# How softmax inverses reach the row layout in an attention and expert kernel: one 128x8 transpose and a broadcast through DRAM in place of a widened transpose

## The chip, the core and the metric

One Trainium2 chip, one of its NeuronCores. The metric is the device time of one execution, in microseconds (us), median of several runs. The kernel before takes 1382.95 us (three runs, 1381.9 to 1384.7).

## The reference, cut to what matters

`x` is 8 batches of 512 tokens with 256 features. A layer norm is followed by two branches whose results are both added to `x`: a mixture of 32 experts, and a latent attention with 16 heads. Only the attention matters here:

```python
scores = einsum('bhqd,bhkd->bhqk', query, key) * scale      # causal
attn = softmax(scores, axis=-1)
out = einsum('bhqk,bhkd->bhqd', attn, value)                # value = norm_kv @ W_dv
return out.transpose(0, 2, 1, 3).reshape(B, S, NH * VD) @ W_o
```

The kernel multiplies by the latent `norm_kv` (64 wide) in place of the value, and folds `W_dv` and `W_o` into one matrix. The division by the sum of a row's exponentials is done after that product, so each head and query needs one number, 1 / (row sum).

## The kernel before, in words

**Stages.** `attention` projects all batches and then runs `heads_first` on batches 0 to 3. `experts` follows, then `heads_last` on batches 4 to 7. The two head stages have the same build, in 32 pairs of heads each, and the change touches only them.

**A step.** Both stages run a pipeline of steps `g`, one head each, 16 to a batch, with `TAIL` = 6 more at the end. Every engine walks the same steps through its own `step` function, in an order written out by hand. `bt.back(g, lag)` names the head that was `lag` steps ago. There is no planner: an engine works through its own list, and a wait at its head holds all behind it.

- TensorE in step `g`: scores of query tile 3 (512 keys), in even steps the six matmuls of `queries` for the next pair, scores of tile 2, in odd steps `turn_norms` and `values` of the pair that ended two steps ago, scores of tile 1, then `turn` (ten 128x128 transposes of the head before, L1149 and L1587), scores of tile 0. In four even steps of a batch (4, 6, 12, 14) a `piece` of the output product with 24 matmuls runs first.
- VectorE: the four `maxima` of the step, and in even steps, between the first two, `between`: half of the rotated queries, `latent_norm` of the pair four steps ago (L1315, L1778), and the reciprocals `inverses` (L1303, L1766).
- ScalarE: the four `exps`, in even steps `queries_latent` behind the first of them (two 64x512 copies out of PSUM bank 0, L1217 and L1669, counted by `q_abs`), then the other copies.
- GpSimd: indirect DMAs (a scatter of token rows in the first stage, a gather with addition in the last). In the first stage also `latent_lo` (L1073).
- SyncE: the loads of the next batch's queries and latents and the stores of results (`during`). Behind batch 1 it also stores the weights (L1039 to L1041) and loads the first expert weights (L878, L879).

**The work around the change.** `rinv` holds the inverses as 128 queries x (2 heads, 4 query tiles). The product in PSUM, `o_ps`, has its rows by head and latent feature (2 x 64) and its columns by query (512), so the inverses must be turned and repeated over 64 rows. Before, GpSimd (first stage, L1078) or ScalarE (last stage, L1688) widens them to 128x512 in `spread`, TensorE turns `spread` with four 128x128 transposes (L1135, L1573) into bank 0, and ScalarE copies these 128x512 to `norms` (L1236, L1695). VectorE then multiplies `o_ps` by `norms`.

Bank 0 of PSUM is also where `queries` puts the first half of a pair's queries. So `turn_norms` waits until ScalarE has copied these out of it:

```python
pe.wait_ge(q_abs, min(NH * b + 2 * p + 6, NH * HB))
```

`2 * p + 6` is the count behind pair `p + 2`. Before, `turn_norms` of pair `p` runs in step `2p + 3`, one step after that copy.

## Time and profile before

| | |
|---|---|
| median of three runs | 1382.95 us |
| the profiled execution, its time and its span | 1381.9 us, 1381.9 us |
| TensorE busy | 1291.0 us (93%) |
| VectorE, ScalarE, GpSimd busy | 61%, 62%, 45% |
| `heads_first` | from 187.5 to 607.6 us |
| `experts` | from 608.6 to about 957 us |
| `heads_last` | from 957 us to the end |
| one pair of heads without a piece | 11.0 us |
| mean granted clock of TensorE | 0.981 of full speed |

The profile is of one execution, and all its times count from the span's start. Engines: PE is the matmul part of TensorE, PEld its weight loads, DVE VectorE, ACT ScalarE, POOL GpSimd, SP SyncE. An added q (SPq) marks what an engine's queue issues, as a DMA. A merged row of the timeline gives the start of its first instruction, the time that they cover, and their number.

### The profile page before, as it was taken

What the parts mean: (1) busy time and instruction counts of PE and PEld (TensorE: products, weight loads), DVE (VectorE), ACT (ScalarE), POOL (GpSimd) and SP (SyncE); (2) the same over time, 40 slices, a digit from 0 to 9 for tenths busy, and PEclk for the clock granted to TensorE, in tenths of its full rate; (3) what the DMA queues carried; (4) which work ended last, traced back from release to release, by engine and by line L of the source; (5) the groups of instructions that cost most, each with busy time, mean ns of one, the idle gap of its engine ahead of it and who ended that gap; (6) DMA issues with size and microseconds to landing.
All of it is one profiled execution on the core that took longest, in us unless ns stands there. A gap on an engine that the chain in (4) does not pass through costs nothing. (4 is left out here: it accounts for less than half of the span.)

```text
span 1381.9 us, 24599 instructions
## 1 busy us (share of the span) xinstructions
PE 1291.0 (93%) x7384; PEld 959.9 (69%) x7385; DVE 844.4 (61%) x3207; ACT 858.4 (62%) x2326; POOL 617.0 (45%) x542
## 2 busy tenths in 40 slices
PE   4999769999999999969999999997999999999997
PEld 3666446767777667757788888886667767777765
DVE  4587678777777677723333333333777777777774
ACT  1455427776677577635556656664777777777673
POOL 1111117777775777710000000001888888887820
PEclk9899979999999999999999999998999999999999
DMA  9977653333327422259976666664565665765510
GB/s 342 392 281 275 253 228 114 101 106 111 115 98 256 162 95 92 85 155 316 329 232 188 188 183 190 188 186 126 100 92 87 129 99 90 132 104 89 97 28 31
DMA packets 147284, 223.28 MB, mean 162 GB/s; under 512 B 13846, under 2 KB 128214, under 8 KB 142294
## 3 DMA queue, kind: packets, MB, share of 16 engines
q1 hardware_dynamic: 99350, 157.72, 33.9%
q0 software_dynamic: 36864, 53.50, 18.9%
q10 hardware_dynamic: 10944, 10.49, 2.6%
q8 instruction: 65, 1.06, 0.3%
q14 instruction: 61, 0.50, 0.1%
HBM read 105.27 MB, written 116.39 MB: 160 GB/s over the span
## 5 line engine op out<-in xcount | busy, mean ns | idle before, releaser
L1523 POOL DMA_INDIRECT l_sums<-sorted_y,slot_no x192 | 300.1, 1563 | 424.7 <-DMA l_sums<-base_dram 366.9
L1068 POOL DMA_INDIRECT sorted_x<-f_xn_row,slot_no x192 | 204.7, 1066 | 49.2 <-issue 44.5
L1224 ACT ACTIVATE f_prob<-f_prob,f_negmax 128x512 f32<-128x512 f32 (+3 forms) x256 | 142.6, 557 | 121.3 <-DVE f_negmax L1297 110.8
L2075 DVE SCALAR_TENSOR_TENSOR act_f<-hidden,rows_in,ps 128x96 f32<-128x96 f32 x224 | 70.5, 315 | 231.1 <-ACT hidden L2038 231.0
L1676 ACT ACTIVATE l_prob<-l_prob,l_negmax 128x512 f32<-128x512 f32 (+3 forms) x256 | 141.7, 555 | 104.9 <-DVE l_negmax L1760 97.2
L2000 PE MATMUL ps<-wgu_sb,xt_e 128*128 x896 | 184.2, 328 | 0.5 <-issue 0.4
L1565 PE MATMUL ps<-l_kt,l_qt 128*128 128x512 f32 (+3 forms) x512 | 170.5, 447 | 5.4 <-DVE l_qt L1751 4.8
L1127 PE MATMUL ps<-kt_s,f_qt 128*128 128x512 f32 (+3 forms) x512 | 170.8, 448 | 5.0 <-DVE f_qt L1288 4.4
L1297 DVE CUSTOM_DVE_ANT_0 f_prob<-ps,mask_add 128x512 f32<-128x512 f32 (+3 forms) x256 | 121.0, 486 | 83.5 <-issue 82.5
L1760 DVE CUSTOM_DVE_ANT_0 l_prob<-ps,mask_add 128x512 f32<-128x512 f32 (+3 forms) x256 | 121.0, 486 | 81.0 <-issue 79.7
L2000 PEld LDWEIGHTS ps<-wgu_sb,xt_e 128*128 128x128 f32 x896 | 139.9, 190 | 3.0 <-issue 2.0
L2018 PE MATMUL ps<-wd_sb,at 96*128 x448 | 139.3, 392 | 1.1 <-issue 0.6
L2046 ACT ACTIVATE rows_out<-ps 128x256 f32<-128x256 f32 x224 | 86.0, 384 | 81.4 <-PE ps L2018 81.3
L1127 PEld LDWEIGHTS ps<-kt_s,f_qt 128*128 128x128 f32 x512 | 82.7, 191 | 42.6 <-DVE f_negmax L1297 10.3
L1565 PEld LDWEIGHTS ps<-l_kt,l_qt 128*128 128x128 f32 x512 | 82.7, 191 | 42.5 <-DVE l_negmax L1760 11.9
L2033 ACT ACTIVATE xt_e<-ps 128x256 f32<-128x256 f32 x224 | 84.7, 378 | 19.2 <-PE ps L1989 19.1
L1989 PE MATMUL ps<-ident,rows_in 128*128 128x128 f32 x448 | 86.4, 274 | 7.6 <-DMA rows_in<-sorted_x 4.7
L2038 ACT ACTIVATE hidden<-ps 128x96 f32<-128x96 f32 x224 | 56.3, 251 | 51.4 <-PE ps L2000 51.4
L1989 PEld LDWEIGHTS ps<-ident,rows_in 128*128 128x128 f32 x448 | 62.1, 141 | 33.1 <-DMA rows_in<-sorted_x 8.2
L1587 PE MATMUL ps<-ident,l_prob 128*128 128x128 f32 x640 | 80.4, 273 | 1.6 <-ACT l_prob L1676 1.6
L1149 PE MATMUL ps<-ident,f_prob 128*128 128x128 f32 x640 | 80.4, 273 | 1.4 <-ACT f_prob L1224 1.4
L1149 PEld LDWEIGHTS ps<-ident,f_prob 128*128 128x128 f32 x640 | 73.9, 141 | 8.0 <-ACT f_pt L1230 1.6
(194 smaller groups left out, 2660.6 us busy)
## 6 DMA issues: line engine op xcount, KB each, us to landing
sorted_x<-zeros SPq DMA_DIRECT2D x14, 2304.0 KB, 9.8
rows_in<-sorted_x SPq DMA_DIRECT2D x112, 288.0 KB, 3.1
sorted_y<-rows_out SPq DMA_DIRECT2D x112, 256.0 KB, 2.1
wgu_sb<-in_wgu SPq DMA_DIRECT2D x16, 384.0 KB, 5.2
x_in<-in_x SPq DMA_DIRECT2D x8, 512.0 KB, 10.3
xn_dram<-xn SPq DMA_DIRECT2D x8, 512.0 KB, 4.0
base_dram<-x_in SPq DMA_DIRECT2D x8, 512.0 KB, 2.9
nqt_dram<-nqt_out SPq DMA_DIRECT2D x8, 512.0 KB, 3.9
```

Of the source, the lines that this page charges most:

```text
L1068: pool.indirect_dma_start(sorted_x, bass.IndirectOffsetOnAxis(ap=slot_no[:, t, k:k + 1], axis=0), xn_row[buf][:], None).then_inc(scattered ...
L1127: mm = pe.matmul(s_ps[k % 2][:, 0:w], qt[g // 2 % 2][g % 2][:, n * P:w], kt_s[:, b, 0:w], start=True, stop=True)
L1149: mm = pe.transpose(pt_ps[:, at:at + P], prob[:, g % 2, qt_no, kt_no * P:(kt_no + 1) * P], ident[:])
L1224: act.activation(prob[:, i, qt, 0:w], prob[:, i, qt, 0:w], ACT.Exp, bias=negmax[:, i, qt:qt + 1], scale=-1.0, accum_out=rowsum[:, g // 2 % ...
L1297: dve.tensor_tensor_reduce(prob[:, i, qt, 0:w], s_ps[k % 2][:, 0:w], mask[:, S - w:S], -1.0, -MASKED, ALU.add, ALU.min, negmax[:, i, qt:qt ...
L1523: pool.indirect_dma_start(sums[n % NSUM][:, t, :], None, sorted_y, bass.IndirectOffsetOnAxis(ap=slot_no[:, TT * GROUPS[n] + t, k:k + 1], a ...
L1565: mm = pe.matmul(s_ps[k % 2][:, 0:w], qt[g // 2 % 2][g % 2][:, n * P:w], kt[b - HB][:, 0:w], start=True, stop=True)
L1676: act.activation(prob[:, i, qt, 0:w], prob[:, i, qt, 0:w], ACT.Exp, bias=negmax[:, i, qt:qt + 1], scale=-1.0, accum_out=rowsum[:, g // 2 % ...
L1760: dve.tensor_tensor_reduce(prob[:, i, qt, 0:w], s_ps[k % 2][:, 0:w], mask[:, S - w:S], -1.0, -MASKED, ALU.add, ALU.min, negmax[:, i, qt:qt ...
L1989: mm = pe.transpose(xt_ps[par][:, kc * P:(kc + 1) * P], rows_in[j // 2 % AHEAD][:, par, kc * P:(kc + 1) * P], ident[:])
L2000: mm = pe.matmul(gu_ps[1 - par], xt[1 - par][:, kc, :], wgu_sb[kc][:, bass.ds(owner, 1), :].rearrange("p a f -> p (a f)"), start=kc == 0, ...
L2018: pe.matmul(y_ps[1 - par], at[1 - par][:], wd_sb[:, bass.ds(owner, 1), :].rearrange("p a h -> p (a h)"), start=True, stop=True)\
```

## The change

The inverses are turned as they are, `rinv` being 128x8, by one transpose into 8 partitions x 128 columns. ScalarE copies these to `inverse` (8 x 128). SyncE stores them in DRAM (4 KB), waits for the landing, waits until VectorE has read the `norms` of the pair before, and loads them with two broadcasting DMAs, 64 rows of 2 KB each, into `norms`. The widening is gone from GpSimd and from ScalarE. `turn_norms` stands one step earlier, in the even step behind the scores of tile 1 and ahead of `turn`. ScalarE's copy moves likewise, behind the third `exps` of the even step. SyncE's list is now written by steps, so its other DMAs have set places: the queries' loads in steps 5 and 13, the latents' in 11 and in 3 of the next batch, `x_res` in 15, the store of `res` in 7 of the next batch, and the stores of the weights with the first expert weights in step 7 of batch 2.

```diff
@@ both stages: tiles
-    spread = sb("f_spread", [P, 2, TT, 2, KVR])
+    inverse = sb("f_inverse", [2 * TT, 2, P])
-    norms_ps = ps[:, 0, :]
+    norms_ps = ps[0:2 * TT, 0, 0:P]
@@ both stages: SyncE, in place of during(b)
+            def spread_inverses(b, p):
+
+                sp.wait_ge(norms_copied, NP_ * b + p + 1)
+                sp.dma_start(norms_dram[p % 2], inverse[:, p % 2, :]).then_inc(norms_stored, 16)
+                sp.wait_ge(norms_stored, 16 * (NP_ * b + p + 1))
+
+                sp.wait_ge(lat_normed, NP_ * b + p)
+                for i in range(2):
+                    sp.dma_start(norms[i * KVR:(i + 1) * KVR, :].rearrange("r (t q) -> r t q", t=TT),
+                                 norms_dram[p % 2, i * TT:(i + 1) * TT, :].unsqueeze(0).to_broadcast([KVR, TT, P]))\
+                        .then_inc(norms_loaded, 16)
+
+            def step(bt, g):
+                b, p = bt.now, g // 2
+                if g % 2 == 0 and bt.back(g, 2):
+                    spread_inverses(bt.back(g, 2)[0], bt.back(g, 2)[1] // 2)
...
+                if bt.last is not None and g == 7:
+                    sp.wait_ge(res_added, 4 * bt.last + 4)
+                    sp.dma_start(base_dram[bass.ds(TT * bt.last, TT)].rearrange("t p h -> p t h"), res[:])\
+                        .then_inc(res_stored, 16)
+                if b == 2 and bt.last is not None and g == 7:
+                    for k in range(2):
+                        sp.dma_start(wq_dram[k], wq_s[k][:].bitcast(F32)).then_inc(kept, 16)
+                        sp.dma_start(wvo_dram[k], wvo_s[k][:].bitcast(F32)).then_inc(kept, 16)
+                    sp.dma_start(rope_dram, rope_t[:]).then_inc(kept, 16)
+                    for n in range(weights.EARLY):
+                        weights.load_chunk(sp, n, wgu, wd)
...
@@ GpSimd (first stage) and ScalarE (last stage): spread_inverses and its calls are gone
@@ both stages: TensorE
             def turn_norms(b, p):
 
                 pe.wait_ge(q_abs, min(NH * b + 2 * p + 6, NH * HB))
-                pe.wait_ge(spread_ready, NP_ * b + p + 1)
-                for t in range(TT):
-                    mm = pe.transpose(norms_ps[:, t * P:(t + 1) * P],
-                                      spread[:, p % 2, t].rearrange("p i n -> p (i n)"), ident[:])
-                mm.then_inc(norms_turned, 1)
+                pe.wait_ge(rinv_ready, NP_ * b + p + 1)
+                pe.transpose(norms_ps, rinv[:, p % 2].rearrange("p i t -> p (i t)"), ident[:]).then_inc(norms_turned, 1)
...
                 if par == 1 and bt.back(g, 3):
                     b, h = bt.back(g, 3)
-                    turn_norms(b, h // 2)
                     values(b, h // 2)
                 if g < NH:
                     scores(bt.now, g, 2)
+                if par == 0 and bt.back(g, 2):
+                    b, h = bt.back(g, 2)
+                    turn_norms(b, h // 2)
                 if bt.back(g, 1):
                     turn(*bt.back(g, 1))
@@ both stages: ScalarE
             def copy_norms(b, p):
 
                 act.wait_ge(norms_turned, NP_ * b + p + 1)
-                act.wait_ge(lat_normed, NP_ * b + p)
-                act.activation(norms[:], norms_ps, ACT.Copy).then_inc(norms_copied, 1)
+                if NP_ * b + p > 1:
+
+                    act.wait_ge(norms_stored, 16 * (NP_ * b + p - 1))
+                act.activation(inverse[:, p % 2, :], norms_ps, ACT.Copy).then_inc(norms_copied, 1)
@@ both stages: VectorE, latent_norm
-                dve.wait_ge(norms_copied, NP_ * b + p + 1)
+                dve.wait_ge(norms_loaded, 32 * (NP_ * b + p + 1))
```

## Rows read from the trace of the kernel before

**Rows 1.** The page's busy times: engine, us, share of the span, instructions.

```profile
PE 1291.0 (93%) x7384; PEld 959.9 (69%) x7385; DVE 844.4 (61%) x3207; ACT 858.4 (62%) x2326; POOL 617.0 (45%) x542
```

**Rows 2.** Busy time by stretch: PE, PEld, DVE, ACT, POOL, clock, DMA share, GB/s.

```profile
300.00:400.00 100.00, 100.00 (x597) 71.67 (x596) 76.25 (x282) 69.58 (x179) 74.17 (x82) 1.00 0.32 107
```

**Rows 3.** The timeline of PE in an odd step of the first stage.

```profile
343.54 0.81 PE L1127 MATMUL ps<-kt_s,f_qt 128*128 128x384 f32 x2
344.18 0.60 PE L1135 MATMUL ps<-ident,f_spread 128*128 128x128 f32 x4
344.71 2.37 PE L1164 MATMUL ps<-f_pt,f_nkv 128*64 128x512 f32 x16
```

**Rows 4.** The groups by line and form: count, busy us, mean ns, idle before.

```profile
L1149 PE MATMUL ps<-ident,f_prob 128*128 128x128 f32 x640 | 80.4, 273 | 1.4 <-ACT f_prob L1224 1.4
L1149 PEld LDWEIGHTS ps<-ident,f_prob 128*128 128x128 f32 x640 | 73.9, 141 | 8.0 <-ACT f_pt L1230 1.6
...
L1164 PEld LDWEIGHTS ps<-f_pt,f_nkv 128*64 128x64 f32 x512 | 34.3, 138 | 40.5 <-issue 36.0
```

**Rows 5.** The timeline of an even step of the first stage.

```profile
339.83 0.72 ACT L1224 ACTIVATE f_prob<-f_prob,f_negmax 128x512 f32<-128x512 f32 x1 [0.48 <-DVE f_negmax L1297]
...
340.55 1.19 ACT L1217 ACTIVATE f_qt<-ps 64x512 f32<-64x512 f32 x2
...
341.15 0.19 DVE L1303 RECIPROCAL f_rinv<-f_rowsum 128x8 f32<-128x8 f32 x1
...
341.36 1.25 PE L1149 MATMUL ps<-ident,f_prob 128*128 128x128 f32 x10
```

**Rows 6.** The timeline of the last stage's last even step with `queries`.

```profile
1340.74 1.19 ACT L1669 ACTIVATE l_qt<-ps 64x512 f32<-64x512 f32 x2
...
1341.54 1.25 PE L1587 MATMUL ps<-ident,l_prob 128*128 128x128 f32 x10
```

**Rows 7.** The timeline at the end of the first stage, where PE waits for ACT.

```profile
589.46 0.19 ACT L1224 ACTIVATION_READ_ACCUMULATOR f_prob<-f_prob,f_negmax 128x1 f32 x1
...
589.79 1.28 PE L1149 MATMUL ps<-ident,f_prob 128*128 128x128 f32 x10 [1.40 <-ACT f_prob L1224]
```

**Rows 8.** The timeline: the end of an even step's third `exps`, and the next pair's multiplication.

```profile
342.88 0.19 ACT L1224 ACTIVATION_READ_ACCUMULATOR f_prob<-f_prob,f_negmax 128x1 f32 x1
...
351.58 0.69 DVE L1315 TENSOR_TENSOR f_lat<-ps,f_norms 128x512 f32<-128x512 f32 x1
```

**Rows 9.** The DMA issues: count, KB each, median us to landing.

```profile
rows_in<-sorted_x SPq DMA_DIRECT2D x112, 288.0 KB, 3.1
sorted_y<-rows_out SPq DMA_DIRECT2D x112, 256.0 KB, 2.1
```

**Rows 10.** SP's queue, behind batch 1.

```profile
426.81 0.37 SPq L1033 DMA_DIRECT2D base_dram<-f_res  x1
...
437.01 3.43 SPq L878 DMA_DIRECT2D wgu_sb<-in_wgu  x2
...
441.99 1.57 SPq L1022 DMA_DIRECT2D f_nqt<-nqt_dram  x1
```

**Rows 11.** The timeline of batch 2: `turn` in step 6, `latent_norm` in step 10.

```profile
429.15 1.25 PE L1149 MATMUL ps<-ident,f_prob 128*128 128x128 f32 x10
...
450.40 0.69 DVE L1315 TENSOR_TENSOR f_lat<-ps,f_norms 128x512 f32<-128x512 f32 x1
```

**Rows 12.** Busy time by stretch, columns as in rows 2, as the weights' transfers end.

```profile
454.00:456.00 2.00, 0.20 (x1) 0.00 (x0) 2.00 (x8) 1.55 (x6) 1.67 (x3) 1.00 1.04 398
456.00:458.00 2.00, 1.30 (x8) 0.76 (x10) 1.08 (x2) 0.64 (x2) 1.67 (x4) 1.00 0.37 141
458.00:460.00 2.00, 2.00 (x10) 0.85 (x8) 0.00 (x0) 0.48 (x1) 1.60 (x2) 0.54 0.26 82
```

**Rows 13.** The waits from 440 to 470 us: total us, times, longest.

```profile
PE ps L1135 <- POOL f_spread L1078: 2.5, 1, 2.5
```

**Rows 14.** The timeline of the last stage's tail.

```profile
1363.40 0.20 DVE L1766 RECIPROCAL l_rinv<-l_rowsum 128x8 f32<-128x8 f32 x1 [0.52 <-ACT l_prob L1676]
```

More of the change, by code:

```diff
@@ new lines, in step @@
+            def step(bt, g):
+                b, p = bt.now, g // 2
+                if g % 2 == 0 and bt.back(g, 2):
+                    spread_inverses(bt.back(g, 2)[0], bt.back(g, 2)[1] // 2)
+                if b < HB - 1:
+                    if g == 5:
+                        sp.wait_ge(q_ready, 2 * (NP_ * b + QUART))
+                        sp.dma_start(nqt[0][:].bitcast(F32), nqt_dram[b + 1]).then_inc(nqt_loaded[0], 16)
+                    if g == 11:
+                        sp.wait_ge(pv_ready, NP_ * b + QUART)
+                        sp.dma_start(nkv[0][:], nkv_dram[b + 1]).then_inc(nkv_loaded[0], 16)
+                    if g == 13:
+                        sp.wait_ge(q_ready, 2 * (NP_ * b + NP_))
+                        sp.dma_start(nqt[1][:].bitcast(F32), nqt_dram[b + 1]).then_inc(nqt_loaded[1], 16)
+                    if g == 15:
+                        sp.wait_ge(res_added, 4 * b + 2)
+                        sp.dma_start(x_res[:], base_t[b + 1]).then_inc(xres_loaded, 16)
+                if bt.last is not None and g == 3:
+                    sp.wait_ge(pv_ready, NP_ * bt.last + NP_)
+                    sp.dma_start(nkv[1][:], nkv_dram[b]).then_inc(nkv_loaded[1], 16)
+                if bt.last is not None and g == 7:
[9 more added lines that the diff above has]
+                        weights.load_chunk(sp, n, wgu, wd)
@@ L1265, in step @@
                     exps(bt.now, g, 2)
+                if par == 0 and bt.back(g, 2):
+                    b, h = bt.back(g, 2)
+                    copy_norms(b, h // 2)
                 if bt.back(g, 1):
@@ L1506, in _, with spread_inverses @@
-            for b in range(HB, B - 1):
-                during(b)
+            def spread_inverses(b, p):
+                sp.wait_ge(norms_copied, NP_ * b + p + 1)
+                sp.dma_start(norms_dram[p % 2], inverse[:, p % 2, :]).then_inc(norms_stored, 16)
+                sp.wait_ge(norms_stored, 16 * (NP_ * b + p + 1))
+                sp.wait_ge(lat_normed, NP_ * b + p)
+                for i in range(2):
+                    sp.dma_start(norms[i * KVR:(i + 1) * KVR, :].rearrange("r (t q) -> r t q", t=TT),
+                                 norms_dram[p % 2, i * TT:(i + 1) * TT, :].unsqueeze(0).to_broadcast([KVR, TT, P]))\
+                        .then_inc(norms_loaded, 16)
@@ new lines, in step @@
+            def step(bt, g):
+                b, p = bt.now, g // 2
+                if g % 2 == 0 and bt.back(g, 2):
+                    spread_inverses(bt.back(g, 2)[0], bt.back(g, 2)[1] // 2)
+                if b < B - 1:
+                    if g == 5:
+                        sp.wait_ge(q_ready, 2 * (NP_ * b + QUART))
+                        sp.dma_start(nqt[0][:].bitcast(F32), nqt_dram[b + 1]).then_inc(nqt_loaded[0], 16)
+                    if g == 11:
+                        sp.wait_ge(pv_ready, NP_ * b + QUART)
+                        sp.dma_start(nkv[0][:], nkv_dram[b + 1]).then_inc(nkv_loaded[0], 16)
+                    if g == 13:
+                        sp.wait_ge(q_ready, 2 * (NP_ * b + NP_))
+                        sp.dma_start(nqt[1][:].bitcast(F32), nqt_dram[b + 1]).then_inc(nqt_loaded[1], 16)
+                if bt.last is not None and g == 3:
+                    sp.wait_ge(pv_ready, NP_ * bt.last + NP_)
+                    sp.dma_start(nkv[1][:], nkv_dram[b]).then_inc(nkv_loaded[1], 16)
+                if bt.last is not None and g == 7:
+                    store_out(bt.last)
@@ L1508, in _ @@
+            pipeline(step)(sp)
             store_out(B - 1)
@@ L1570, in turn_norms @@
                 pe.wait_ge(q_abs, min(NH * b + 2 * p + 6, NH * B))
-                pe.wait_ge(spread_ready, NP_ * b + p + 1)
-                for t in range(TT):
-                    mm = pe.transpose(norms_ps[:, t * P:(t + 1) * P],
-                                      spread[:, p % 2, t].rearrange("p i n -> p (i n)"), ident[:])
-                mm.then_inc(norms_turned, 1)
+                pe.wait_ge(rinv_ready, NP_ * b + p + 1)
+                pe.transpose(norms_ps, rinv[:, p % 2].rearrange("p i t -> p (i t)"), ident[:]).then_inc(norms_turned, 1)
             def turn(b, g):
@@ L1634, in step @@
                     b, h = bt.back(g, 3)
-                    turn_norms(b, h // 2)
                     values(b, h // 2)
@@ L1638, in step @@
                     scores(bt.now, g, 2)
+                if par == 0 and bt.back(g, 2):
+                    b, h = bt.back(g, 2)
+                    turn_norms(b, h // 2)
                 if bt.back(g, 1):
@@ L1727, in step @@
                     exps(bt.now, g, 2)
+                if par == 0 and bt.back(g, 2):
+                    b, h = bt.back(g, 2)
+                    copy_norms(b, h // 2)
                 if bt.back(g, 1):
```

85 lines of the change are left out of this document (17 added, 68 removed).

## The prediction, made before the changed kernel was run

> **What bounds the kernel now.** I read the page first: TensorE's matmul part is busy for 93% of the span [rows 1]. The busy time by stretch then shows that in the middle of a head stage it is busy for all of 100 us, at full clock, with every other engine below 77% [rows 2]. So in the steady part of both head stages only what stands in TensorE's own list costs time. Work taken from ScalarE or GpSimd gives nothing there, unless TensorE waits for it. The timeline of one odd and one even step then gives prices for what leaves and enters that list.
>
> **What is removed.** In an odd step the last matmul of the scores ahead, two of 0.32 each from 343.54, ends its streaming at 344.18. Four transposes follow, and `values` starts at 344.71: 0.53 us from start to start [rows 3]. Ten such transposes take 1.25 us with 273 ns for one alone [rows 4, 5], so in a row each costs (1.25 - 0.27) / 9 = 0.109 us, and four cost 0.44. The other 0.09 is the change to `values`' 64-column tiles, which stays. I take 0.44 (bounds 0.44 and 0.53). There are 32 pairs in each stage, and in two of the 64 the odd step belongs to a tail: 62 x 0.44 = 27.3 us less. The widening on GpSimd and ScalarE, and ScalarE's 128x512 copy lie beside TensorE: nothing.
>
> **What is added, and the wait that comes with it.** `turn_norms` now stands in the even step, in the place where `turn` starts today. It still waits for the count `2 * p + 6` of `q_abs`. Before, that copy was one step old. Now it is the copy of the same step: pair `p + 2` is the one whose queries TensorE has just computed. ScalarE's two copies end at 340.55 + 1.19 = 341.74, and `turn` starts at 341.36 [rows 5]: TensorE would come 0.38 us too early. In the last pair of the last stage it is 1340.74 + 1.19 - 1341.54 = 0.39 [rows 6]. Of the 60 pairs with a copy in such a step, all but one have 0.38 to 0.40. The copies can't come earlier: they stand behind the first `exps`, which waits for VectorE's maximum [rows 5], and that for the scores. The reciprocals are done at 341.34, ahead of the copies. Where TensorE does wait for ScalarE, it starts 589.79 - 589.65 = 0.14 us behind the release [rows 7]. The transpose itself then delays `turn` by its weight load, 0.14 [rows 4], since nothing runs that could cover it. Together 0.38 + 0.14 + 0.14 = 0.66 us for each of 60 pairs, 39.6 us; the two pairs without queries cost one transpose each, 0.2 in all. Bounds: 0.52 if the transpose is free, 0.79 if its whole 0.27 is exposed. The steady part so gives 39.6 + 0.2 - 27.3 = **+12.5 us** (between -1 and +21).
>
> Row and rule differ on that weight load. A load of 64 columns takes 138 ns and one of 128 takes 141 [rows 4], so for 8 columns I keep 0.14. The Trainium skill, "TensorE: Matmul & The Clock Gate", section "LDWEIGHTS (loading the stationary operand)", has it proportional to the columns. By that, 8 columns would cost nearly nothing; an estimate from it is 0.1 us less in each of 60 pairs, and a sum 6 us lower.
>
> **The new path of the inverses.** ScalarE's small copy would start when the third `exps` ends, 343.07 [rows 8]. It has a quarter of the columns of a 0.59 us copy; I take 0.25 (bounds 0.19, as for one column, and 0.59). SyncE then stores: 0.14 for the release and 2.1 to landing, loads: 0.14, the second issue 0.37, and 3.1 to landing [rows 9, 10]. That is 343.32 + 2.24 + 3.61 = 349.2. VectorE multiplies at 351.58 [rows 8]. So 2.4 us are left, and the trip is hidden (0), even though both prices are of transfers of 256 KB and more. Its cover is that slack; beyond it every microsecond stalls VectorE, behind which stand the other maxima, and so TensorE. GpSimd's transfers share the DMA engines; 256 KB per 11 us adds a few per cent.
>
> **SyncE's list.** Every other DMA of it moves to a set step. The loads of queries, latents and `x_res` come one to four steps later than today and are used steps after that: nothing. One place costs. In batch 2 the store of `res` and eleven large DMAs follow each other from 426.81; they are issued until 442 and single issues take over 1 us, where a free queue takes 0.37 [rows 10]. That is a queue filled to its end. It is drained at about 456.5 [rows 12]: 29.7 us for 7.9 MB, by the sizes of the tiles. In the changed kernel SyncE gets to them only behind the inverses of pair 2: `turn` at 429.15 [rows 11], the third `exps` ends 1.71 later as in rows 5 and 8, then copy, store and the issue of two loads, 434.1. Two loads (0.63 MB) are no longer in the block, so it takes 27.3 us, to 461.4. The store of pair 3's inverses is issued behind all that. I take it to land when the queue is empty, and the loads 3.6 later, at 465.0. They are due at 450.40 [rows 11]: TensorE stands for 14.6 us. Behind such a stop its clock falls: after today's short one it is 0.54 [rows 12], about 2 us lost. But today's stop, 2.5 us for GpSimd's late widening [rows 13] and its 2 us at the low clock, goes with the widening. So 14.6 + 2 - 4.5 = **+12 us** (lower bound -4, if the small store passes the block; upper +20).
>
> **Tails.** Reciprocals at 1363.60 [rows 14], transpose and copy to 1364.3, landing by the same prices at 1370.2; today VectorE multiplies at 1368.2, so up to 2 us, and about 1 in the first stage. The prices are for larger transfers, so I take half, **+1.5 us** (0 to 4).
>
> **Sum.** 1381.9 + 12.5 + 12 + 1.5 = 1407.9 us for the profiled execution. It was 1.05 below the median of the runs, so 1409.
>
> **Rivals.**
> - *The copies no longer arrive late: faster.* With 0.44 us less in each odd step the engines could settle so that `q_abs` is there in time. Then a pair gives 0.44 for 0.14 spent: 60 x 0.30 = 18 us less, and with 12 and 1.5 the time is 1378. It decides in the even step between the second scores and `turn`: the sum is a gain once TensorE's added time there is under 0.22 us in place of 0.66. For it: TensorE is the bound. Against it: the chain of scores, maximum, `exps`, copies has only idle time of 0.48 ahead of `exps` that its own maximum ends [rows 5], and it starts from TensorE's own scores, so it shifts with them. Chance 0.12.
> - *The trip through DRAM is longer than its cover: much slower.* If landing took 8.3 us from the copy on, in place of 5.9, every further microsecond would come 60 times; with loads of 6.2 us in place of 3.1, 0.7 x 60 = 42 us more, about 1450. For it: 64 rows read the same 2 KB of DRAM, which no row shows. Against it: the slack above. The Trainium skill, "DMA: Bandwidth & Descriptors", section "Rules for kernel authors", speaks against transfers under 64 KB as mostly overhead; it prices none that would outlast this slack. Chance 0.09.
> - *The wait costs 0.4 and the block nothing*, so that all cancels: 1383 to 1386. Chance 0.05.
>
> **Numbers.** The forecast has a chance of 0.72, and its own range is 1392 to 1425, from the bounds of the wait and of the block, not all at their ends together. Some 0.02 is for gains that I don't see. The range, 1376 to 1425, takes in the faster rival. A measurement here can tell about 0.2% from no change. Faster 0.14, within 0.2% 0.05, slower 0.81.
>
> **What would show it.** In the timeline of an even step: TensorE idle for some 0.5 us ahead of one transpose, released by ScalarE's `f_qt`; the stretch at 100 us no longer all busy; a pair at 11.2 us in place of 11.0. In batch 2: one stop of over 10 us in which VectorE waits for the load of `norms`, and a low clock behind it. No idle TensorE ahead of `turn_norms` would prove the steady part wrong; waits of `latent_norm` for DMAs in most pairs would mean the second rival; no long stop near 450 to 465 us would take 12 us off.

## The result, and the profile after

The kernel after takes 1406.56 us (median of four runs, 1405.16 to 1411.24), the kernel before, beside it, 1383.83 us (four runs, 1381.9 to 1387.33). The ratio is 1.0164, 95% interval 1.0142 to 1.0186: slower by 22.7 us. Forecast were 1409 us, in a range of 1376 to 1425. The profiled execution took 1405.44 us, with a span of 1403.7.

The page's busy times of the kernel after, beside [rows 1]:

```profile
PE 1283.7 (91%) x7193; PEld 930.6 (66%) x7193; DVE 847.1 (60%) x3207; ACT 826.4 (59%) x2294; POOL 593.9 (42%) x510
```

TensorE has 191 matmul records fewer, 32 x 2 x 3 = 192 being the transposes removed. Its work shrank and its time grew, so the new time is idle time. The busy time by stretch, for the window of [rows 2]:

```profile
300.00:400.00 100.00, 97.73 (x568) 66.68 (x567) 75.98 (x276) 66.27 (x177) 66.21 (x73) 1.00 0.37 128
```

In the stretch that was busy for 100 us, TensorE now stands for 2.3 us, at full clock. The timeline of an even step (the one of [rows 5]) shows where. Columns: start, us, engine, line, operation, tiles, count; in brackets the idle time ahead of it and its releaser.

```profile
341.31 1.19 ACT L1228 ACTIVATE f_qt<-ps 64x512 f32<-64x512 f32 x2
341.91 0.19 DVE L1316 RECIPROCAL f_rinv<-f_rowsum 128x8 f32<-128x8 f32 x1
...
342.55 0.08 PEld L1146 LDWEIGHTS ps<-ident,f_rinv 128*8 128x8 f32 x1 [0.67 <-ACT f_qt L1228]
342.55 0.27 PE L1146 MATMUL ps<-ident,f_rinv 128*8 128x128 f32 x1 [0.27 <-ACT f_qt L1228]
...
342.66 1.28 PE L1158 MATMUL ps<-ident,f_prob 128*128 128x128 f32 x10
```

The query copies end at 342.50, the inverses were ready at 342.10, and the transpose starts 0.05 behind the copies: the wait that was forecast, released by the engine that was forecast. PE's row shows only 0.27 us of idle time, because a record runs on past the place where the next matmul could start: in the kernel before, that of the scores ahead ends 0.17 behind the start of `turn` (341.53 and 341.36). Together 0.44, which to rounding is the 0.38 that TensorE would come too early and the 0.05 of the release. The waits of the whole kernel (total us, times, longest) count it in 59 of the 60 pairs that have a copy in that step:

```profile
PEld ps L1604 <- ACT l_qt L1700: 20.4, 30, 0.7
PEld ps L1146 <- ACT f_qt L1228: 19.4, 29, 0.7
DVE f_lat L1328 <- DMA f_norms<-norms_dram: 16.7, 2, 13.6
```

The third line is the stop in batch 2, with 3.1 us in the first stage's tail beside it; in no steady pair does VectorE wait for the DMA. The timeline of that stop, beside [rows 10, 11]:

```profile
448.47 1.26 SPq L880 DMA_DIRECT2D wd_sb<-in_wd  x1
449.77 1.48 SPq L1023 DMA_DIRECT2D norms_dram<-f_inverse  x1
462.66 1.09 SPq L1028 DMA_DIRECT2D f_norms<-norms_dram  x2
...
466.37 0.69 DVE L1328 TENSOR_TENSOR f_lat<-ps,f_norms 128x512 f32<-128x512 f32 x1 [13.63 <-DMA f_norms<-norms_dram]
...
467.31 0.37 PE L1146 MATMUL ps<-ident,f_rinv 128*8 128x128 f32 x1 [13.57 <-DVE f_rinv L1316]
```

The 4 KB store is issued as the last of the block. SyncE may issue the two loads only when it has landed, 12.9 us later, when the large transfers are through. VectorE stands for 13.63 us, TensorE for nearly as long. The busy time by stretch there, columns as in rows 2:

```profile
455.00:460.00 5.00, 0.00 (x0) 0.00 (x0) 0.00 (x0) 0.00 (x0) 2.91 (x3) 0.70 1.02 369
460.00:465.00 5.00, 0.00 (x0) 0.00 (x0) 0.00 (x0) 0.00 (x0) 3.36 (x5) 0.50 0.62 217
465.00:470.00 5.00, 2.69 (x13) 2.68 (x14) 1.64 (x8) 1.61 (x6) 0.00 (x0) 0.50 0.14 48
470.00:475.00 5.00, 5.00 (x27) 2.47 (x26) 4.03 (x15) 3.04 (x8) 0.85 (x1) 0.94 0.23 79
```

TensorE does nothing for 13.6 us, from 453.7 to 467.3, and comes back at half its clock (0.50, the 1.2 GHz level).

**The ledger.** I measure a pair from the end of ScalarE's second query copy to the next such end. The table has the most frequent value for pairs without a piece, "short pairs"; the others in this stage were 13.67 and are 13.80. From the first to the 32nd such end, the first stage is 15.4 us longer (378.0 to 393.4): 10.5 in the pair with the stop (28.68 for 18.0, where its like went from 13.67 to 13.80), 4.8 in all others. The last stage is 2.7 us longer (381.1 to 383.8), the time behind its last copy 4.3 (39.95 to 44.25). The rest, between and ahead of the stages, is 0.6 less. Together 21.8 us of span. In that rest stands `experts`, which neither the change nor any experiment touches: from its first matmul to its last it took 344.3 us before and 346.3 after, and 342.8 to 348.3 in the thirteen profiled executions. So the spans of two profiled executions can differ by some us for no reason of the edit, and the lengths of the pairs tell more.

### The profile page after: what moved, and what is told of

Read it like the earlier page. It is cut to its first block and busy times, and to the rows that moved or that the text cites. A ratio compares the mean times of both kernels' runs of the same rounds, so it can differ in the third digit from the quotient of the medians.

```text
span 1403.7 us, 24406 instructions
## 1 busy us (share of the span) xinstructions
PE 1283.7 (91%) x7193; PEld 930.6 (66%) x7193; DVE 847.1 (60%) x3207; ACT 826.4 (59%) x2294; POOL 593.9 (42%) x510
## 5 line engine op out<-in xcount | busy, mean ns | idle before, releaser
L1555 POOL DMA_INDIRECT l_sums<-sorted_y,slot_no x192 | 305.0, 1588 | 423.8 <-DMA l_sums<-base_dram 365.9
L1089 POOL DMA_INDIRECT sorted_x<-f_xn_row,slot_no x192 | 201.3, 1048 | 49.1 <-issue 44.5
L1094 POOL TENSOR_TENSOR f_lat_lo<-f_lat,f_lat_hi 128x512 fp32r<-128x512 f32 x32 | 48.3, 1509 | 83.5 <-ACT f_lat_hi L1254 83.4
```

Source lines behind the costliest of these rows:

```text
L1089: pool.indirect_dma_start(sorted_x, bass.IndirectOffsetOnAxis(ap=slot_no[:, t, k:k + 1], axis=0), xn_row[buf][:], None).then_inc(scattered ...
L1555: pool.indirect_dma_start(sums[n % NSUM][:, t, :], None, sorted_y, bass.IndirectOffsetOnAxis(ap=slot_no[:, TT * GROUPS[n] + t, k:k + 1], a ...
```

## The experiments

The kernel before, measured beside each group, had medians of 1383.8 us (the kernel after and experiments 1 to 4), 1383.5 (5 to 8), 1385.2 (9) and 1384.5 (10). Lengths of short pairs come from the traces.

| kernel | median us | ratio to before (95%) | short pair, first stage | last stage |
|---|---|---|---|---|
| before | 1383.8 | 1 | 11.03 | 11.02 |
| after | 1406.56 | 1.0164 (1.0142 to 1.0186) | 11.27 | 11.16 |
| the wait alone | 1407.89 | 1.0184 (1.0152 to 1.0216) | 11.52 | 11.52 |
| one transpose of four | 1372.58 | 0.9915 (0.9885 to 0.9944) | 10.92 | 10.79 |
| transpose behind `turn` | 1385.97 | 1.0011 (0.9994 to 1.0028) | 10.82 | 10.70 |
| block spread | 1393.12 | 1.0077 (1.0048 to 1.0107) | 11.27 | 11.16 |
| both repairs | 1371.72 | 0.9917 (0.9894 to 0.9940) | 10.83 | 10.70 |
| transpose inside `turn`, block spread | 1368.61 | 0.9894 (0.9872 to 0.9916) | 10.82 | 10.69 |
| before, block spread | 1385.17 | 1.0009 (0.9992 to 1.0026) | 11.03 | 11.02 |
| one transpose in the odd step, block spread | 1399.04 | 1.0098 (1.0059 to 1.0137) | 10.71 | 10.4 to 12.3 |
| `latent_lo` behind the scatters | 1426.36 | 1.0288 (1.0263 to 1.0313) | 11.16 or 11.27 | 11.16 |
| the same with the transpose inside `turn` | 1396.20 | 1.0079 (1.0062 to 1.0096) | 10.71 | 10.70 |
| a short `latent_lo`, block spread | 1390.07 | 1.0042 (1.0026 to 1.0059) | 11.16 | 11.16 |

### 1. The wait alone, in the kernel before

```diff
                 if g < NH:
                     scores(bt.now, g, 2)
+                if g > 1 and par == 0 and bt.next_pair(p):
+                    nb, np_ = bt.next_pair(p)
+                    pe.wait_ge(q_abs, NH * nb + 2 * np_ + 2)
                 if bt.back(g, 1):
                     turn(*bt.back(g, 1))
```

> The kernel before, and in it alone that TensorE waits, ahead of turn in every even step that has queries, for ScalarE's copies of these queries; it does nothing with what it waited for. Theory (the wait for q_abs is the price of the change): the copies end 0.38 us behind the place and the release costs 0.05 to 0.14, so 60 x 0.43 to 0.52 = 26 to 31 us more, about 1410 us, and a pair without a piece takes 11.5 us in place of 11.03. Rival (such a wait is absorbed by slack elsewhere, the loss comes from the DMAs): 1383 us, pairs at 11.0.

Measured: 24 us more than before, with nothing else changed, a little under the 26 to 31 expected. A pair costs 0.49 us more in both stages. The edit leaves out step 0 of each batch (`g > 1`), and there six pairs keep their 11.0 us; the pair that had the stop in the kernel before takes 16.8 in place of 18.0. The timeline shows the same release at the same place:

```profile
344.99 1.19 ACT L1220 ACTIVATE f_qt<-ps 64x512 f32<-64x512 f32 x2
...
346.23 1.07 PEld L1149 LDWEIGHTS ps<-ident,f_prob 128*128 128x128 f32 x10 [0.67 <-ACT f_qt L1220]
346.23 1.31 PE L1149 MATMUL ps<-ident,f_prob 128*128 128x128 f32 x10 [0.27 <-ACT f_qt L1220]
```

So waiting for ScalarE's query copies ahead of `turn` costs its length in nearly every pair; no other work makes up for it. That 24 us is close to the 22.7 of the change is chance: in the change, the wait is set against the 0.44 us that the odd step saves, and the stop and the last tail come on top.

### 2. One transpose of four, in the kernel before

```diff
-                for t in range(TT):
+                for t in range(1):
                     mm = pe.transpose(norms_ps[:, t * P:(t + 1) * P],
```

> The kernel before with only the first of the four transposes of turn_norms; left out are the three others, so three quarters of the inverses are not turned. Theory (TensorE's list is the bound of both head stages): three transposes at 0.109 us in 62 odd steps, 20 us less, about 1363 us, pairs at 10.7 us. Rival (VectorE's chain behind the maxima bounds the odd step as closely): less than 10 us gained.

This leaves three quarters of the inverses unturned. Measured: 11.2 us less, where 20 follow from 62 times three transposes, and under 10 from the rival. In the profiled executions the two head stages give 13.4 us, and `experts` takes 3.1 longer. Pairs with a piece give what three transposes cost, 0.33 us (13.67 to 13.35). Short pairs give 0.11 in the first stage and 0.23 (some 0.33) in the last. In the first stage the missing part is a new wait of the scores for VectorE's sum of the rotated queries: in the kernel before,

```profile
PEld ps L1127 <- DVE f_qt L1288: 5.3, 2, 3.6
```

and with one transpose

```profile
PEld ps L1127 <- DVE f_qt L1288: 9.9, 16, 3.6
```

The sum comes late because it has itself grown longer. TensorE's shorter odd step has moved it onto GpSimd's `latent_lo`:

```profile
344.10 1.26 POOL L1073 TENSOR_TENSOR f_lat_lo<-f_lat,f_lat_hi 128x512 fp32r<-128x512 f32 x1 [0.37 <-ACT f_lat_hi L1241]
...
345.02 0.89 DVE L1288 TENSOR_TENSOR f_qt<-f_qa,f_qb 64x512 f32<-64x512 f32 x1
```

In the kernel before it took 0.69 us and began when `latent_lo` ended. In the two short pairs of this run in which the two don't meet (from 209.3 and from 435.9), the sum takes 0.69 and the pair 10.72, which is all but 0.02 of the 0.33. So TensorE's list is the bound, and the 0.2 us that most short pairs lack come from the meeting of VectorE and GpSimd (experiments 9 and 10 take this up). I had not seen in a stretch of 100% busy time that an engine so close behind could be pushed into the way. What the last stage's 10.79 waits for, where `latent_lo` does not run, is not shown.

### 3. The transpose behind turn, in the kernel after

```diff
                 if g < NH:
                     scores(bt.now, g, 2)
+                if bt.back(g, 1):
+                    turn(*bt.back(g, 1))
                 if par == 0 and bt.back(g, 2):
                     b, h = bt.back(g, 2)
                     turn_norms(b, h // 2)
-                if bt.back(g, 1):
-                    turn(*bt.back(g, 1))
@@ ScalarE likewise: copy_norms behind turned
```

> The changed kernel with turn_norms behind turn in the even step, and ScalarE's copy of the inverses behind its copy of the turned tiles. The copies of the queries are then long done. Theory: of the 0.54 us that an even step gained, 0.43 are the wait and go: 60 x 0.43 = 26 us under the changed kernel's 1406.6, about 1381 us, pairs at 10.8 us in both stages; the stop in batch 2 (over 10 us) stays. The trip through DRAM starts 1.3 us later and must still end in time. Rival (the loss is in the trip through DRAM): 1407 us or, as the trip starts later, more.

Measured: the pairs fall from 11.27 and 11.16 to 10.82 and 10.70 us, 0.45 each, and the time by 20.6 us to that of the kernel before. Everything else of the change is still in it, the stop too. So the wait is the whole loss of the steady part, and the place one line further down avoids it. The two stages give the expected 26 us in the profiled executions (13.5 and 12.5); the first stage's tail takes 3.5 us of them back, 43.7 in place of 40.2 from the last query copy to the first expert matmul. The price is a later trip, as the waits show:

```profile
DVE f_lat L1328 <- DMA f_norms<-norms_dram: 20.4, 3, 14.7
DVE l_lat L1802 <- DMA l_norms<-norms_dram: 15.1, 12, 4.7
```

The longest of the first line is the stop, and 5.1 us of it and 4.7 us of the second stand in the two tails. What is left in the last stage, 10.4 us in 11 waits beside GpSimd's gather, does not show in the pairs: they stay at 10.70 us.

### 4. The block spread, in the kernel after

```diff
-                if b == 2 and bt.last is not None and g == 7:
-                    for k in range(2):
-                        sp.dma_start(wq_dram[k], wq_s[k][:].bitcast(F32)).then_inc(kept, 16)
...
+                n = NH * (b - 2) + g - 7
+                if 0 <= n < 4:
+                    to, of = ((wq_dram, wq_s), (wvo_dram, wvo_s))[n % 2]
+                    sp.dma_start(to[n // 2], of[n // 2][:].bitcast(F32)).then_inc(kept, 16)
...
```

> The changed kernel with the eleven large DMAs of SyncE in batch 2 (weights stored, first expert weights loaded) put one to a step from step 7 on, in place of all in step 7. Theory: the store of a pair's inverses then waits behind at most two of them (2 MB, about 6 us of an 11 us pair), so the stop of 13.6 us and the half clock behind it go: 10 to 14 us under 1406.6, about 1394 us, waits of VectorE for the load of norms in batch 2 and 3 together under 3 us. Rival (the transfers' bytes, not their place in the queue, cause the stop): the same time lost in several smaller waits, 1404 to 1407.

Measured: 13.4 us less than the kernel after, all of it in one place: the pair with the stop takes 14.89 in place of 28.68 us, and the other pairs keep their length. In batch 2 the multiplication no longer waits for the DMA at all. The one wait left in the stage is in its tail, at 596.6 us, where the kernel after has 3.1:

```profile
DVE f_lat L1335 <- DMA f_norms<-norms_dram: 3.2, 1, 3.2
```

The pair is still 1.1 us over its like. There GpSimd, held up by the loads of its token rows, runs `latent_lo` inside VectorE's sum, which takes 2.08 us in place of 0.69, and TensorE's piece waits 0.9 us for `latent_lo`.

### 5. Both repairs

The edits of 3 and 4 together:

```diff
+                if bt.back(g, 1):
+                    turn(*bt.back(g, 1))
                 if par == 0 and bt.back(g, 2):
...
+                n = NH * (b - 2) + g - 7
+                if 0 <= n < 4:
```

> The two repairs together: the transpose of the inverses behind turn (with ScalarE's copy behind turned), and batch 2's eleven large DMAs one per step instead of one block. Theory: the two costs lie in different stretches (every even step; batch 2's steps 8 to 10), so the gains add. The transpose behind turn alone gave 1386.0 with its stop of some 15 us still in it, the spread block alone took away 13.4 us of 1406.6. Together 1386.0 - 13.4 = 1372.6 us, below the kernel before's 1383.8: pairs of 10.82 us in the first stage and 10.70 in the last, and no pair of over 15 us in batch 2. Rival: with the transpose late, the trip through DRAM has nearly no slack, and the large transfers, now spread over eleven steps, push each of its landings behind the multiplication: then several pairs of batch 2 grow by 1 us or more and it stays at 1380 or above.

Measured 1371.72 us, 0.9 from the sum: the two gains add. One part of the expectation failed: a pair in batch 2 takes 15.74 us, 2.4 over its like. It is not the rival's late landing. The multiplication does not wait for the DMA there; TensorE's piece waits 2.2 us for `latent_lo`. The DMA's waits in the last stage (15.8 us, 11 times, 4.9 of it in the tail) don't show in the pairs there, which keep 10.70.

### 6. The transpose inside turn, block spread

```diff
                 for qt_no in range(TT):
+                    if qt_no == TT - 1 and between:
+                        turn_norms(between[0], between[1] // 2)
```

> As the spread block, but the transpose of the inverses stands inside turn, ahead of its last four transposes, and ScalarE's copy where the change has it. Six transposes of some 0.125 us cover the wait for the query copies (0.54 us behind the place of the change). Theory: the wait is gone as with the transpose behind turn (pairs of 10.8 and 10.7 us), but the inverses start their trip some 0.5 us or more sooner, so the last stage's waits of the multiplication for the DMA (15.1 us in 12 waits with the transpose behind turn) are mostly gone: 1367 to 1372 us. Rival (the trip is hidden anyway, and those waits cost nothing but in the tail): the same as the kernel with both repairs to 2 us, 1370 to 1374. Rival against both: the break in the chain of ten transposes costs TensorE as much as the wait did: 1385 or more.

Measured 1368.61 us (1367.75 to 1370.42), 14.9 below the kernel before: the fastest. Its timeline:

```profile
335.55 1.19 ACT L1237 ACTIVATE f_qt<-ps 64x512 f32<-64x512 f32 x2
...
336.36 0.82 PE L1167 MATMUL ps<-ident,f_prob 128*128 128x128 f32 x6
...
337.01 0.27 PE L1153 MATMUL ps<-ident,f_rinv 128*8 128x128 f32 x1
...
337.12 0.60 PE L1167 MATMUL ps<-ident,f_prob 128*128 128x128 f32 x4
```

Six transposes of `turn` run while ScalarE finishes (336.74), and the one for the inverses follows without a gap. It costs its 0.11 us and nothing more. The waits for the DMA in the last stage fall to 6.4 us in 4, of which 3.9 in the tail. Against both repairs the time is 3.1 us less, but the two intervals overlap and the pairs are alike, so I don't claim a difference. The busy time by stretch is nearly what [rows 2] showed:

```profile
300.00:400.00 100.00, 99.83 (x584) 69.10 (x584) 79.10 (x289) 69.36 (x187) 69.11 (x75) 1.00 0.39 130
```

### 7. The block spread in the kernel before

The same spreading of the eleven DMAs, in SyncE's list of the kernel before, two of them behind each pair's `values`, with the next batch's loads set between them:

```diff
-            for n in range(weights.EARLY):
-                weights.load_chunk(sp, n, wgu, wd)
-            for b in range(2, HB - 1):
-                during(b)
+            for n in range(5 + 3 * weights.EARLY):
+                if n % 2 == 1:
+                    sp.wait_ge(pv_ready, 2 * NP_ + 3 + n // 2)
...
```

> The kernel before, with its own eleven large DMAs spread over the steps of batch 2 in the same way: the control for the part of the repair that has nothing to do with the change. Before, the pair under the block took 18.0 us against 13.7 for its like, 4.3 more. Theory: 4 us less, 1379 to 1381 us, so that of the spread block's 13.4 us some 9 to 10 belong to the change. Rival: the gain is the clock's and the weights' contention, and as large here as in the changed kernel, 10 us or more (1372): then the change is charged too much for its stop.

Measured: no gain; both theories were wrong. The pair under the block takes 16.09 us in place of 18.0, but a later one 15.58 in place of 13.67: the 4.3 us are still lost, in two places. GpSimd's widening is now late twice, and the pieces wait twice for `latent_lo`, as the waits from 440 to 520 us show:

```profile
PE ps L1156 <- POOL f_spread L1099: 1.8, 2, 0.9
PE ps L63 <- POOL f_lat_lo L1094: 1.7, 2, 1.1
```

So in the kernel before the spreading is worth nothing: what the block holds up there is GpSimd, and that moves with the transfers. The 13.4 us in the changed kernel belong to the small store behind the block, which the kernel before doesn't have.

### 8. One transpose in the odd step, block spread

The transpose, ScalarE's copy and SyncE's part go back to the odd step, where the four transposes stood:

```diff
                 if par == 1 and bt.back(g, 3):
                     b, h = bt.back(g, 3)
+                    turn_norms(b, h // 2)
                     values(b, h // 2)
                 if g < NH:
                     scores(bt.now, g, 2)
-                if par == 0 and bt.back(g, 2):
-                    b, h = bt.back(g, 2)
-                    turn_norms(b, h // 2)
```

> As the spread block, but the one transpose, ScalarE's copy and SyncE's part are back in the odd step, where the kernel before had its four: no wait for the query copies at all. Theory: pairs 10.6 to 10.7 us in the first stage by TensorE alone (0.41 less than before), but the trip starts some 5.5 us ahead of the multiplication (which stands in the next even step) and measured 4.6 to 5.3 us with the copy ahead of it: it is hidden by under 1 us, and where a landing comes late VectorE waits for it and the scores behind it too. If hidden: 1368 to 1372. Rival: the trip is longer than the cover in most pairs, and each wait of VectorE is paid in full: over 200 us-hundredths a pair, pairs of 11.2 or more and 1385 or above. The sign between 1372 and 1385 tells whether the change's early place bought anything.

Measured 1399.04 us (1389.93 to 1402.94): the rival, if less evenly than it said. The undisturbed pairs of the first stage are 10.71 us, and that stage takes 375.0 us, 4.7 less than with the block spread alone (379.7). The loss is in the last stage, 394.0 in place of 384.9. The waits there, and one trip:

```profile
DVE l_lat L1805 <- DMA l_norms<-norms_dram: 54.1, 32, 4.5
```

```profile
1009.01 0.27 SPq L1515 DMA_DIRECT2D norms_dram<-l_inverse  x1
1011.24 1.11 SPq L1520 DMA_DIRECT2D l_norms<-norms_dram  x2
...
1014.85 0.69 DVE L1805 TENSOR_TENSOR l_lat<-ps,l_norms 128x512 f32<-128x512 f32 x1 [0.69 <-DMA l_norms<-norms_dram]
```

From the store's issue to the multiplication it takes 5.8 us here, and the multiplication waits in all 32 pairs, against 20 in the first stage. Here is the second rival of the prediction, the trip that outlasts its cover: with the one transpose in the old place it is real. The move to the even step is what hides the trip; only its exact line was wrong.

### 9. latent_lo behind the scatters, twice

In the first stage the short pairs of the kernel after are 0.11 us longer than in the last. GpSimd's `latent_lo` overlaps there with VectorE's sum of the rotated queries, since TensorE's shorter odd step moved the two together. `latent_lo` now also starts while VectorE's product `f_qb` ahead of the sum is still running:

```profile
347.53 0.69 DVE L1295 TENSOR_TENSOR f_qb<-f_qb,rope_t 128x512 f32<-128x512 f32 x1
347.82 1.54 POOL L1094 TENSOR_TENSOR f_lat_lo<-f_lat,f_lat_hi 128x512 fp32r<-128x512 f32 x1 [0.91 <-ACT f_lat_hi L1254]
...
349.10 0.80 DVE L1301 TENSOR_TENSOR f_qt<-f_qa,f_qb 64x512 f32<-64x512 f32 x1
```

It starts 0.41 us ahead of the end of `f_qb` and takes 1.54 us in 28 such pairs, where it takes 1.27 in the four that don't meet it. So it is still running when the sum starts, 1.28 us behind it (the 0.9 of the first text below is too small), and the sum takes 0.80 in place of 0.69.

```diff
+                if g < NH:
+                    scatter(TILES * bt.now + p, par)
                 if par == 1 and bt.back(g, 5):
                     b, h = bt.back(g, 5)
                     latent_lo(b, h // 2)
-                if g < NH:
-                    scatter(TILES * bt.now + p, par)
```

> As the spread block (1393.1 us), but GpSimd's latent_lo of the first stage stands behind its three scatters instead of ahead of them. In the changed kernel it starts 0.9 us ahead of VectorE's last sum of the rotated queries and runs beside it, that sum takes 738 ns in place of 687 in the mean, and the scores of the next pair wait for it. Theory: this overlap is why the first stage's short pairs grew by 0.24 us and the last stage's by 0.13: here they are 11.16 us as in the last stage, 17 x 0.11 = 1.9 us less, 1391 us, and GpSimd's 128x512 subtraction falls back from 1.51 us to about 1.27. Rival: the 0.11 us has another cause (VectorE's order of work around latent_norm): pairs stay 11.27 and the time 1393.

> As the kernel with the transpose inside turn (1368.6 us, pairs of 10.82 us in the first stage and 10.69 in the last), with GpSimd's latent_lo behind its scatters. Theory as for the run beside it: the first stage's short pairs come down to 10.70, 17 x 0.12 = 2 us less, 1366 to 1367 us. Rival: 10.82 again and 1368 to 1369. A third way: moved back, latent_lo delays the pieces of the output product that wait for it, and the pairs with a piece grow over 13.35.

Measured: 1426.36 and 1396.20 us, 33 and 28 us slower than the kernels that they start from; the move is no repair. Behind the scatters, `latent_lo` inherits their wait for token rows (99.7 us in 28 waits in the first of the two), and the pieces wait for it (19.6 us in 8 waits, against 4.4 in 2 with the block spread alone): in the first kernel the pairs ahead of them go from 13.80 to some 15.2, two of them to 19.4 and 23.4. The third way of the second text was right, and I had not put it in the first. In the steps that the scatters don't hold up, a short pair is 11.27 where the two instructions meet as above, and 11.16 where they stay apart or meet at a later sum, which speaks for the theory within one run. Where `latent_lo` starts inside the sum, a short pair is 12.8 to 13.0:

```profile
262.62 2.42 DVE L1308 TENSOR_TENSOR f_qt<-f_qa,f_qb 64x512 f32<-64x512 f32 x1
...
263.20 1.28 POOL L1101 TENSOR_TENSOR f_lat_lo<-f_lat,f_lat_hi 128x512 fp32r<-128x512 f32 x1
```

VectorE's sum takes 2.42 us in place of 0.69 around GpSimd's 1.28.

### 10. A short latent_lo, block spread

```diff
-                pool.tensor_tensor(lat_s[1][:, q, :], lat[:, q % 2, :], lat_s[0][:, q, :].bitcast(F32),
+                pool.tensor_tensor(lat_s[1][:, q, 0:8], lat[:, q % 2, 0:8], lat_s[0][:, q, 0:8].bitcast(F32),
```

> As the spread block (1393.1 us), but GpSimd's latent_lo subtracts 8 of its 512 columns; the rest of the low part of the latents stays zero, so that part of the first stage's output product is left out (its matmuls run as before). All other work, order and waits are the same. The two orders tried before moved latent_lo and made other things wait; this one only makes it short. Theory: the overlap with VectorE's sum of the rotated queries is what the first stage's short pairs lose beyond the wait: the sum takes 0.69 us in every pair, the short pairs are 11.16 us as in the last stage, and the 15 of them that were 11.27 give 1.7 us, 1391 us. Rival: something else in the first stage's steps costs the 0.11, and the pairs stay 11.27.

Measured: every short pair of the first stage's steady part is 11.16 us, and the sum takes 687 ns in the mean, by the groups of lines of this kernel

```profile
L1309 DVE TENSOR_TENSOR f_qt<-f_qa,f_qb 64x512 f32<-64x512 f32 x64 | 43.9, 687 | 2.0
```

and of the kernel after:

```profile
L1301 DVE TENSOR_TENSOR f_qt<-f_qa,f_qb 64x512 f32<-64x512 f32 x64 | 47.2, 738 | 2.0
```

The theory holds: the overlap is the 0.11 us. The first stage is 1.3 us shorter than with the block spread (378.4 and 379.7). The medians differ by more, 1390.07 and 1393.12, and against the kernel before beside each by 5.6 and 9.3 us; but the intervals of the two ratios overlap, and 2.1 us of the profiled difference are in the last tail, which the edit doesn't touch. So the time does not confirm the 1.7 us; the pairs and the sum do.

## Why the prediction was right, point by point

**What bounds the kernel.** Right: TensorE's list sets the pair. What I missed is that a shorter list moves other engines against each other. GpSimd's `latent_lo` then meets VectorE's sum of the rotated queries, and this holds the scores up, by 0.2 us in experiment 2 and by 0.11 in the kernel after.

**Removed, 0.44 us a pair.** Right. A short pair of the last stage is 10.69 us with the one transpose inside `turn` (6), 0.33 under the kernel before, and that one transpose costs 0.11. In the first stage the pairs of experiment 9 in which `latent_lo` keeps clear of the sum are 10.70 to 10.71 too.

**The wait, 0.66 us.** The mechanism, its place, its engine and its count (60; 59 seen) were right, and experiments 1 and 3 show it from both sides. Its size was 0.54: `turn` starts 3.41 us behind the start of its pair's queries, against 2.87 before. Two terms were too large. The release cost 0.05 us and not the 0.14 of [rows 7]. The transpose delayed `turn` by 0.11 (342.55 to 342.66) and not by 0.14; that is the step of 0.109 between transposes in a row, whose loads take 141 ns, so the length of the load was the wrong price. The last stage's pairs confirm it: +0.54 - 0.41 (what the odd step gave in the trace of after) = +0.13, and they grew by 0.14.

**Row against rule on the weight load.** The loads of the two transposes, by the groups by form:

```profile
L1604 PEld LDWEIGHTS ps<-ident,l_rinv 128*8 128x8 f32 x32 | 2.7, 83 | 22.4 <-ACT l_qt L1700 20.4 <-issue 2.0
L1146 PEld LDWEIGHTS ps<-ident,f_rinv 128*8 128x8 f32 x32 | 2.7, 83 | 35.2 <-ACT f_qt L1228 19.4 <-issue 15.7
```

83 ns for 8 columns, beside 138 for 64 and 141 for 128 [rows 4]. Neither was right for the load: my 0.14 was too much, and the proportional rule of the Trainium skill, "TensorE: Matmul & The Clock Gate", section "LDWEIGHTS (loading the stationary operand)", would have nearly nothing.

**The steady sum, +12.5.** It came to +7.5 (4.8 and 2.7), within the bounds of -1 to +21. One term was missing: that TensorE's shift moves `latent_lo` onto VectorE's sum, 0.11 in some 15 short pairs, +1.7 us (10). It hid part of my overestimate, 60 times 0.12 or 7.2 us.

**The trip through DRAM, hidden.** Right in every steady pair. Where no other work was in the way, in the first stage's tail, it took 4.64 us from the store's issue (604.95) to the multiplication (609.59), where the prices of large transfers made 5.85 from the copy's end; under the last stage's gather it took 5.8 (8). The cover is owed to the place: started a step later, the trip costs some 27 us (experiment 8 against 5).

**SyncE's list, +12.** Right, and by the mechanism named: the small store lands behind the block. It was +10.5 in the span of that pair, 14.9 lost against 4.3 before. The stop was 13.6 where 14.6 were forecast, and the clock behind it fell to 0.50. Spreading the block gave back 13.4 us (4), and in the kernel before nothing (7). That the change takes the old stop away, for which I had set off 4.5 us, came true as well.

**Tails, +1.5.** Too small, and for a reason I had not named. From the last query copy to the first expert matmul the first stage's tail got 1.8 us shorter (42.0 to 40.2), where I had some 1 us more, although its multiplication does wait 3.1 us for the DMA. The last tail got 4.3 longer. The timeline of the kernel before there,

```profile
1363.51 1.28 PE L1587 MATMUL ps<-ident,l_prob 128*128 128x128 f32 x10 [1.57 <-ACT l_prob L1676]
...
1365.69 2.37 PE L1602 MATMUL ps<-l_pt,l_nkv 128*64 128x512 f32 x16 [0.46 <-ACT l_pt L1683]
...
1368.17 0.69 DVE L1778 TENSOR_TENSOR l_lat<-ps,l_norms 128x512 f32<-128x512 f32 x1 [0.80 <-PE ps L1602]
```

and of the kernel after:

```profile
1381.05 0.27 PE L1604 MATMUL ps<-ident,l_rinv 128*8 128x128 f32 x1 [1.81 <-DVE l_rinv L1790]
...
1381.36 1.78 PE L1616 MATMUL ps<-ident,l_prob 128*128 128x128 f32 x10
...
1384.03 4.54 PE L1631 MATMUL ps<-l_pt,l_nkv 128*64 128x512 f32 x16 [0.90 <-ACT l_pt L1714]
...
1388.67 0.69 DVE L1802 TENSOR_TENSOR l_lat<-ps,l_norms 128x512 f32<-128x512 f32 x1 [3.45 <-PE ps L1631]
```

The multiplication does not wait for the DMA that I had priced. It waits for `values`, which takes 4.54 us in place of 2.37: TensorE works at 0.50 of its clock from 1382 to 1388, after the idle time of 1.81 us ahead of the transpose. Before, 1.57 us of idle time at the like place left the clock at 1.00. So the traces show that it fell, and not what made the difference.

Eight of the nine profiled kernels with the new path have a last tail of 44.3 to 45.0 us and the ninth (experiment 10) one of 42.7; those without it have 40.0 to 42.0, so it belongs to the change. It comes about in two ways. In the kernel after, the clock holds the multiplication back, to 29.3 us behind the last query copy (26.2 before). With both repairs (5), `values` runs at full clock in 2.37 us, and the multiplication still starts 29.3 us behind that copy, since it waits 4.9 us for the DMA. So taking away one of the two need not shorten this tail. What the trip alone would cost at the place of the change, no run here separates.

**The sum.** Forecast were +26.0 us and the profiled execution has +21.8. The steady part was 5.0 too high and the block 1.5, the last tail 2.8 too low; the rest is 0.6 less. So the time came out 2.4 us from the forecast partly because errors cancelled; the two large terms had the right sign and mechanism.

**The rivals.** The first, that the copies are not late, did not come by itself, and is what the repairs made of it: pairs of 10.7 us. With the stop still in it I had it at 1378 us; experiment 3 is that case and took 1386. Of the difference, 3.6 us are the last tail (5.1 longer than before, where I had 1.5 for both), 1.7 the first stage's (43.7 and 42.0), and 2.0 `experts`, where the edit changes nothing. The third rival, the wait at 0.4 and no block, was wrong in both halves.

## What to carry to other kernels

When work is moved earlier on a full engine, look up the newest event that its old wait stands for: a wait that was one step old can become one for the step's own work, and cost more than the work saved. A place a few instructions further down, behind work that needs nothing new, gives the gain back. After such a shift, compare the lengths of instructions on the other engines too: two that used to follow each other may now meet. A small DMA that the compute waits for belongs ahead of the megabytes in its queue, or these have to be spread.

## What the runs showed of the hardware that I had not expected

- VectorE's and GpSimd's instructions on two tiles in SBUF held each other up. GpSimd's 128x512 subtraction took 1.54 us in place of 1.27 when it started 0.41 ahead of the end of VectorE's product `f_qb`; the same with 8 columns (10) took 0.47 in place of 0.20. VectorE's sum took 0.80 us in place of 0.69 when it started with 0.25 us of the subtraction left, 0.89 with 0.34 left (2), and 2.42 where the subtraction, itself at 1.28, started inside it (9). The Trainium skill, "GPSIMD Engine Reference", section "1. Specifications", names contention with VectorE's instructions that have two SBUF inputs; the traces agree.
- A weight load of 8 columns took 83 ns, one of 64 138 ns and one of 128 141 ns. The next matmul started 0.11 us behind the transpose with 8 columns, as in a row of transposes with 128.
- The release of TensorE by ScalarE took 0.05 us here (342.50 to 342.55, and 346.18 to 346.23 in experiment 1), against 0.14 in [rows 7].
- A store of 4 KB behind 7 MB in SyncE's queue had not landed for 12.9 us, against 1.2 to 2.6 us from its issue to that of the loads in the other 63 pairs. The Trainium skill, "DMA: Bandwidth & Descriptors", section "Two DMAs through the same engine are not ordered", has the descriptors of one queue start in order on a DMA engine; the trace agrees.
